# Attention and feed-forward on one core: from x stored by pairs of tokens to x stored tile by tile

## The chip, the core and the metric

The kernel runs on one core of a Trainium2 chip. The metric is device time in microseconds of one execution. Before the change the median of three runs is 562.25 us (561.91 to 562.63). Nothing leaves the core; its inputs and its output lie in HBM.

## The reference

Eight batches of 1024 tokens with 256 channels, all in fp32. What is computed, cut to what matters:

```
xn = layernorm(x)
q, k, v = split(xn @ qkv_w + qkv_b)          # 16 heads of 16 channels
q, k = l2norm(q), l2norm(k)                  # per head
kv = k^T v                                   # per head, over all tokens of a batch
attn = (q kv) @ proj_w + proj_b
ffn = relu(xn @ W1 + b1) @ W2 + b2           # 256 -> 1024 -> 256
out = x + attn + ffn
```

There is no softmax: attention is linear, so kv and proj_w are folded into one 256 x 256 matrix m per batch, and attention becomes one product of q with m.

## The kernel before, in words

**Products.** Every fp32 value is held as two parts, hi and lo, of the type that TensorE multiplies. `product` (L1097 to L1101) computes hi x hi, hi x lo and lo x hi in three matmuls, so every product below is three matmuls per chunk of 128 channels.

**Halves.** A batch is worked off in two halves of 512 tokens (`half`, s = 0 to 15, u = s mod 2), a half in four tiles of 128 tokens or two pairs of tiles. After both halves of a batch, `end` does the attention of that batch. `all_batches` writes out batch 0 and the last, and loops over those between them. The order of work is written out by hand for each engine; the engines meet through semaphores alone.

**Order of the columns.** x is transposed to channel-major form, in which a row holds one channel and a column one token. x and q are transposed in blocks of 32 x 32 on VectorE and moved by DMA (`move`) into xT_raw and qT_lo. In that form the two tiles of a pair are interleaved: the columns of the first tile are the even ones of the pair, those of the second the odd ones. Two helpers name the two views of 512 such columns: `by_tile` reads them pair, tile, token, with a step of two columns; `in_pairs` reads adjacent columns by the same three counts.

**TensorE per half.**

- `ffn_up` (j = 0 to 7): w_bank gets W1 chunk (stationary) times xT (moving, 512 columns). 6 matmuls.
- `ffn_down`: o_bank gets W2 chunk times h (moving, 512 columns). 6 matmuls. In the last half of all, `ffn_down_last` instead takes a tile of h as the stationary operand and W2 as the moving one, with 256 columns, so that the result is already token-major.
- `query_key` (t = 0 to 3): v_bank gets a tile of xT (stationary) times wqk (moving, 512 columns): q and k of 128 tokens. 6 matmuls. The tile is taken from xT by `of_tile`, every other column of a pair.
- `gather`: g_bank sums xn (stationary) times k (moving, 256 columns), 24 matmuls.

**TensorE per batch.** `key_value` and `project` make m. Then `end` runs `attend` twice (u = 0 into v_bank, u = 1 into o_bank on top of the feed-forward result): stationary m, moving qT, 512 columns, 12 matmuls each. In the last batch `attend` runs once, into w_bank, and `attend_last` uses tiles of qT (by `of_tile`) as stationaries, 256 columns.

**ScalarE and VectorE around them.** `xT_high` (L537, helper line L493) and `xT_low` (helper line L738) split xT_raw. In the opening, `xT_high_pair`, `xT_low_pair`, `xT_high_first` and `xT_low_first` split transposes that TensorE made into banks, and they write every other column to get the interleaved order. `h_high` (L568) and `h_low` (L895) split the result of the first feed-forward layer. `yT_out` (L583) copies o_bank with its bias to yT; `add_attention` (L922) adds v_bank to yT; `spread_y` (L934) transposes yT in blocks of 32 x 32 to token-major y_rows, which needs the interleaved order that the output's DMA undoes.

**Columns that the next engine waits for.** The next half's `query_key` waits for xT_lo; the next half's `ffn_down` at j = 0 waits for yT_copied of its bank; `query_key` with u = 1 waits for yT_added of v_bank.

Of the kernel before, what the change touches and what calls it, by code (L numbers as in the profile page):

```python
# [41 lines left out]
P = 128  # L42
# [20 lines left out]
def build(nc, x, qkv_w, qkv_b, proj_w, proj_b, w1, b1, w2, b2, out):  # L63
# [6 lines left out]
    with ctx:  # L70
# [155 lines left out]
        def xn_of(s):  # L226
            return xn_first[:] if is_second(s) else y_sb[:, 0] if is_third(s) else xn[:]

# [262 lines left out]
        def _(act):  # L491
# [30 lines left out]
            def xT_high_pair(a, k):  # L522

                if a == 0:
                    act.wait_ge(xT_pair_ready, k + 1)
                else:
                    act.wait_ge(xT_ready, k + 1)
                copy(xT_hi[:, 0, k, pair_tokens(a)].rearrange("f (p b) -> f b p", b=PAIR),
                     pair_banks[a][k][:, 0:PAIR * P].rearrange("f (b p) -> f b p", b=PAIR)).then_inc(
                         xT_pair_hi_done if a == 0 else xT_hi_done, 1)  # L530

            def xT_high_first(s, u, k):

                wait(act, xT_ready, KC * s + k + 1)
                copy(by_tile(xT_hi[:, u, k, :]), in_pairs(first_banks[u][k][:])).then_inc(xT_hi_done, 1)

            def xT_high(s, u):  # L537
                wait(act, x_moved, 16 * MOVES * (s - 1))
                for k in range(KC):
                    copy(xT_hi[:, u, k, :], xT_raw[:, k, :]).then_inc(xT_hi_done, 1)  # L540
# [35 lines left out]
            def yT_out(b, u, k):  # L576
# [6 lines left out]
                nc.scalar.activation(yT[u][:, k, :], o_bank[k][:], ACT.Identity,  # L583
# [151 lines left out]
        def _(dve):  # L735
# [106 lines left out]
            def xT_low_pair(a, k):  # L842

                dve.wait_ge(xT_pair_hi_done if a == 0 else xT_hi_done, k + 1)
                to, high = (t[:, 0, k, pair_tokens(a)].rearrange("f (p b) -> f b p", b=PAIR) for t in (xT_lo, xT_hi))
                less(to, pair_banks[a][k][:, 0:PAIR * P].rearrange("f (b p) -> f b p", b=PAIR), high).then_inc(
                    xT_pair_lo_done if a == 0 else xT_lo_done, 1)

            def xT_low_first(s, u, k):

                wait(dve, xT_hi_done, KC * s + k + 1)
                less(by_tile(xT_lo[:, u, k, :]), in_pairs(first_banks[u][k][:]),
                     by_tile(xT_hi[:, u, k, :])).then_inc(xT_lo_done, 1)

            def xT_low(s, u):
                for k in range(KC):
                    wait(dve, xT_hi_done, KC * s + k + 1)
                    less(xT_lo[:, u, k, :], xT_raw[:, k, :], xT_hi[:, u, k, :]).then_inc(xT_lo_done, 1)
# [59 lines left out]
            def add_attention(b, k, last):  # L918
# [3 lines left out]
                nc.vector.tensor_tensor(yT[0][:, k, :], (w_bank if last else v_bank)[k][:], yT[0][:, k, :],  # L922
                                        ALU.add).then_inc(yT_added, 1)
# [172 lines left out]
        def _(pe):  # L1096
# [50 lines left out]
            def query_key(s, u, t, batch=0):  # L1147
# [8 lines left out]
                for k in range(KC):  # L1156
                    done = product(v_bank[t % 2][:],
                                   (of_tile(xT_hi[:, u, k, :], t), of_tile(xT_lo[:, u, k, :], t)),
# [60 lines left out]
            def ffn_down_last(s, batch, j):  # L1219
# [4 lines left out]
                for t in range(TILES):  # L1224
# [4 lines left out]
                    product(to, (of_tile(h_hi[:, r, :], t), of_tile(h_lo[:, r, :], t)),  # L1229
# [158 lines left out]
```

## Time and profile before

| | us |
|---|---|
| median of three runs | 562.25 |
| the profiled execution | 562.05 |
| its span | 560.3 |
| TensorE matmul busy | 554.8 (99%) |
| TensorE weight load busy | 470.3 (84%) |
| VectorE busy | 412.5 (74%) |
| ScalarE busy | 282.5 (50%) |
| GpSimd busy | 116.7 (21%) |

The span runs from the first to the last event of the program; the execution's own time is somewhat longer. The matmul row counts matmuls from their start to a modelled end, and neighbours overlap, so their mean duration is longer than the distance between them. Weight loads (PEld) run beside matmuls.

### The profile page before, as it was taken

Reading aid. Unit: us, or ns where it says so; the run is one execution under the profiler, and the core shown is the slowest. Engines: PE = TensorE matmul, PEld = TensorE weight load, DVE = VectorE, ACT = ScalarE, POOL = GpSimd, SP = SyncE. Lnnn points to the kernel's source line nnn. Section 1 sums busy time; section 2 is a strip of 40 time slices with the busy share of each in tenths; the row PEclk is TensorE's granted clock in tenths of the full one; section 3 lists DMA queues with packets and bytes.
Section 4 is the critical chain, followed back from the end, with each engine's and each line's share of the span. In section 5 each row is a group of like instructions: output and inputs, shape, how many; then the busy total and the mean of one; then the engine's idle time right before and its main releaser. Section 6 shows DMA issues by size and latency. Waiting matters only on the chain.

```text
span 560.3 us, 8965 instructions
## 1 busy us (share of the span) xinstructions
PE 554.8 (99%) x2724; PEld 470.3 (84%) x2724; DVE 412.5 (74%) x810; ACT 282.5 (50%) x518; POOL 116.7 (21%) x148
## 2 busy tenths in 40 slices
PE   9999999999999999999999999999999999999997
PEld 7878888888888888888888888888888888888896
DVE  6787989776785867959668686876778767784745
ACT  3586373556435563365634556445554555433421
POOL 3132421502052020520214202231024300150100
PEclk9999999999999999999999999999999999999999
DMA  8422134343413434034341343414333251324412
GB/s 272 142 82 49 28 81 104 84 104 81 94 25 86 96 85 98 18 85 96 86 89 26 87 96 86 80 35 108 74 88 69 43 106 37 81 33 88 99 39 76
DMA packets 141414, 45.36 MB, mean 81 GB/s; under 512 B 133330, under 2 KB 136402, under 8 KB 141396
## 3 DMA queue, kind: packets, MB, share of 16 engines
q1 hardware_dynamic: 139280, 44.61, 34.8%
q10 hardware_dynamic: 2116, 0.53, 0.5%
q8 instruction: 9, 0.15, 0.1%
q14 instruction: 9, 0.07, 0.1%
HBM read 20.98 MB, written 8.39 MB: 52 GB/s over the span
## 4 chain that ended last, share of the span: by engine, by line
PE 96%; ACT 1%; DVE 1%; DMA 1%; SPq 0%; issue 0%; DVEq 0%
PE o_bank L1101 11%; PE o_bank L1100 11%; PE o_bank L1099 11%; PE w_bank L1099 11%; PE w_bank L1100 10%; PE w_bank L1101 10%; PE v_bank L1099 7%; PE v_bank L1101 7%; PE v_bank L1100 7%; PE g_bank L1101 3%; PE g_bank L1100 3%; PE g_bank L1099 3%; PE kv_bank L1254 1%; DMA y_sb<-w 1%; ACT xn_first L511 0%; PE kv_bank L1256 0%
## 5 line engine op out<-in xcount | busy, mean ns | idle before, releaser
L895 DVE SCALAR_TENSOR_TENSOR h_lo<-w_bank,h_hi 128x512 fp32r<-128x512 f32 x128 | 87.3, 682 | 31.8 <-ACT h_hi L568 30.3
L568 ACT ACTIVATE h_hi<-w_bank 128x512 fp32r<-128x512 f32 x128 | 76.3, 596 | 67.8 <-PE w_bank L1101 66.8
L1099 PE MATMUL w_bank<-xT_hi,w_hi 128*128 128x512 f32 x254 | 100.3, 395 | 0.0
L1100 PE MATMUL w_bank<-xT_lo,w_hi 128*128 128x512 f32 x254 | 99.2, 391 | 0.0
L1101 PE MATMUL w_bank<-xT_hi,w_lo 128*128 128x512 f32 x254 | 98.9, 389 | 0.0
L1101 PE MATMUL o_bank<-h_hi,w_lo 128*128 128x512 f32 x240 | 93.6, 390 | 0.0
L1099 PE MATMUL o_bank<-h_hi,w_hi 128*128 128x512 f32 x240 | 93.4, 389 | 0.0
L1100 PE MATMUL o_bank<-h_lo,w_hi 128*128 128x512 f32 x240 | 93.4, 389 | 0.0
L389 POOL TENSOR_TENSOR xn_lo<-xn,xn_hi 128x256 fp32r<-128x256 f32 x56 | 41.5, 741 | 220.1 <-ACT xn_hi L493 212.7
L404 POOL TENSOR_TENSOR y_sb<-y_sb,y_rows 128x256 f32<-128x256 f32 x56 | 52.2, 936 | 129.0 <-DVE y_rows L934 105.9
L546 ACT ACTIVATE qk_sq<-v_bank 128x512 f32<-128x512 f32 x64 | 38.2, 598 | 77.1 <-PE v_bank L1101 76.6
L862 DVE TENSOR_REDUCE qk_v<-qk_sq 128x32 f32<-128x512 f32 x64 | 43.2, 678 | 35.4 <-ACT qk_sq L546 35.4
L1101 PEld LDWEIGHTS w_bank<-xT_hi,w_lo 128*128 128x128 f32 x254 | 47.7, 188 | 10.5
L1099 PEld LDWEIGHTS w_bank<-xT_hi,w_hi 128*128 128x128 f32 x254 | 47.8, 188 | 9.4 <-DVE h_lo L895 0.3
L1100 PEld LDWEIGHTS w_bank<-xT_lo,w_hi 128*128 128x128 f32 x254 | 47.8, 188 | 8.8
L1099 PEld LDWEIGHTS o_bank<-h_hi,w_hi 128*128 128x128 f32 x240 | 45.1, 188 | 9.5
L1101 PEld LDWEIGHTS o_bank<-h_hi,w_lo 128*128 128x128 f32 x240 | 45.1, 188 | 9.4
L1100 PEld LDWEIGHTS o_bank<-h_lo,w_hi 128*128 128x128 f32 x240 | 45.1, 188 | 9.4
L1099 PE MATMUL v_bank<-wqk_hi,xT_hi 128*128 128x512 f32 x128 | 50.5, 395 | 0.7 <-ACT qk_even L493 0.7
L1101 PE MATMUL v_bank<-wqk_hi,xT_lo 128*128 128x512 f32 x128 | 50.5, 395 | 0.0
L1100 PE MATMUL v_bank<-wqk_lo,xT_hi 128*128 128x512 f32 x128 | 50.4, 394 | 0.0
L511 ACT ACTIVATE xn<-x_sb,ln_offset,ln_rstd 128x256 f32<-128x256 f32 x52 | 27.0, 591 | 29.5 <-DVE ln_offset L790 29.5
(203 smaller groups left out, 984.2 us busy)
## 6 DMA issues: line engine op xcount, KB each, us to landing
qT_lo<-blocks SPq DMA_DIRECT2D x256, 32.0 KB, 1.9
x_sb<-x SPq DMA_DIRECT2D x15, 512.0 KB, 3.7
y_sb<-x SPq DMA_DIRECT2D x60, 128.0 KB, 3.1
out<-y_sb SPq DMA_DIRECT2D x58, 128.0 KB, 2.5
xT_raw<-blocks SPq DMA_DIRECT2D x224, 32.0 KB, 1.9
y_sb<-w SPq DMA_DIRECT2D x4, 256.0 KB, 5.0
x_sb<-x SPq DMA_DIRECT2D x2, 256.0 KB, 2.8
w_raw<-w SPq DMA_DIRECT2D x2, 256.0 KB, 7.0
```

The costliest lines, as they stand in the source:

```text
L389: nc.gpsimd.tensor_tensor(xn_lo[:, u, t, :], xn_of(s)[:, t, :], xn_hi[:, u, t, :].bitcast(F32), ALU.subtract).then_inc(xn_split_done, 1)
L404: nc.gpsimd.tensor_tensor(y_sb[:, u, t, :], y_sb[:, u, t, :], y_rows[:, u, t, :], ALU.add).then_inc(y_done, 1)
L511: done = nc.scalar.activation(to[:, t, :], x_sb[:, u, t, :], ACT.Identity, bias=ln_offset[:, t:t + 1], scale=ln_rstd[:, t:t + 1])
L546: nc.scalar.activation(qk_sq[:, t % 2, :], v_bank[t % 2][:], ACT.Square).then_inc(qk_sq_done, 1)
L568: nc.scalar.activation(h_hi[:, j % RING, :], w_bank[j % 2][:], ACT.Relu).then_inc(h_done, 1)
L862: nc.vector.tensor_reduce(qk_v[:, t, :], qk_sq[:, t % 2, :].rearrange("p (h d) -> p h d", d=D), AXIS.X, ALU.add).then_inc(qk_ss_done, 1)
L895: nc.vector.scalar_tensor_tensor(h_lo[:, r, :], w_bank[j % 2][:], 0.0, h_hi[:, r, :].bitcast(F32), ALU.max, ALU.subtract).then_inc(h_lo_do ...
L1099: nc.tensor.matmul(to, left[0], right[0], start=first, stop=False, skip_group_check=shared)
L1100: nc.tensor.matmul(to, left[0], right[1], start=False, stop=False, skip_group_check=shared)
L1101: return nc.tensor.matmul(to, left[1], right[0], start=False, stop=last, skip_group_check=shared)
L1254: nc.tensor.matmul(kv_raw[:, g, :, :], wv_hi[:, k, heads], g_parts[:, k, :, heads], start=g == 0 and k == 0, stop=False, skip_group_check= ...
```

## The change

xT and h stand tile by tile: the 128 columns of a tile are adjacent. `xT_high` and `xT_low` now read xT_raw by tile and write adjacent columns; in the opening the split writes what the transposes gave without rearranging. `query_key` and `ffn_down_last` take a tile as 128 adjacent columns. Since h, and with it the result of the feed-forward network, now stands tile by tile and qT is still interleaved, `attend` reads its moving operand qT by tile, every other column of a pair. yT is put back in the interleaved order when it is written (`yT_out`), and `add_attention` adds in that order, so `spread_y` and the output's DMA stay as they are. `attend_last` stays as it is. The instructions of every engine are the same, in the same order and of the same size; only their access patterns differ.

```diff
             def xT_high_pair(a, k):
...
-                copy(xT_hi[:, 0, k, pair_tokens(a)].rearrange("f (p b) -> f b p", b=PAIR),
-                     pair_banks[a][k][:, 0:PAIR * P].rearrange("f (b p) -> f b p", b=PAIR)).then_inc(
-                         xT_pair_hi_done if a == 0 else xT_hi_done, 1)
+                copy(xT_hi[:, 0, k, pair_tokens(a)], pair_banks[a][k][:, 0:PAIR * P]).then_inc(
+                    xT_pair_hi_done if a == 0 else xT_hi_done, 1)
...
-                copy(by_tile(xT_hi[:, u, k, :]), in_pairs(first_banks[u][k][:])).then_inc(xT_hi_done, 1)
+                copy(xT_hi[:, u, k, :], first_banks[u][k][:]).then_inc(xT_hi_done, 1)
...
             def xT_high(s, u):
                 wait(act, x_moved, 16 * MOVES * (s - 1))
                 for k in range(KC):
-                    copy(xT_hi[:, u, k, :], xT_raw[:, k, :]).then_inc(xT_hi_done, 1)
+                    copy(in_pairs(xT_hi[:, u, k, :]), by_tile(xT_raw[:, k, :])).then_inc(xT_hi_done, 1)
...
-                nc.scalar.activation(yT[u][:, k, :], o_bank[k][:], ACT.Identity,
+                nc.scalar.activation(by_tile(yT[u][:, k, :]), in_pairs(o_bank[k][:]), ACT.Identity,
                                      bias=bias_T[:, k:k + 1]).then_inc(yT_copied, 1)
...
             def xT_low(s, u):
...
-                    less(xT_lo[:, u, k, :], xT_raw[:, k, :], xT_hi[:, u, k, :]).then_inc(xT_lo_done, 1)
+                    less(in_pairs(xT_lo[:, u, k, :]), by_tile(xT_raw[:, k, :]), in_pairs(xT_hi[:, u, k, :])).then_inc(xT_lo_done, 1)
...
-                nc.vector.tensor_tensor(yT[0][:, k, :], (w_bank if last else v_bank)[k][:], yT[0][:, k, :],
-                                        ALU.add).then_inc(yT_added, 1)
+                to = by_tile(yT[0][:, k, :])
+                nc.vector.tensor_tensor(to, in_pairs((w_bank if last else v_bank)[k][:]), to, ALU.add).then_inc(yT_added, 1)
...
             def query_key(s, u, t, batch=0):
...
-                                   (of_tile(xT_hi[:, u, k, :], t), of_tile(xT_lo[:, u, k, :], t)),
+                                   (xT_hi[:, u, k, tile(t)], xT_lo[:, u, k, tile(t)]),
...
             def ffn_down_last(s, batch, j):
...
-                    product(to, (of_tile(h_hi[:, r, :], t), of_tile(h_lo[:, r, :], t)),
+                    product(to, (h_hi[:, r, tile(t)], h_lo[:, r, tile(t)]),
...
             def attend(b, u, banks):
...
-                                       (qT_hi[:, u, g, :], qT_lo[:, u, g, :]), g == 0 and u == 0, g == KC - 1,
+                                       (by_tile(qT_hi[:, u, g, :]), by_tile(qT_lo[:, u, g, :])), g == 0 and u == 0, g == KC - 1,
```

## Rows read from the trace of the kernel before

**Rows 1.** The page, busy us, share of the span and instructions of each engine
```profile
PE 554.8 (99%) x2724; PEld 470.3 (84%) x2724; DVE 412.5 (74%) x810; ACT 282.5 (50%) x518; POOL 116.7 (21%) x148
```
**Rows 2.** The page, the chain that ended last, shares by engine
```profile
PE 96%; ACT 1%; DVE 1%; DMA 1%; SPq 0%; issue 0%; DVEq 0%
```
**Rows 3.** Waits of PE: who waited for whom, us in total, times, longest
```profile
PE w_bank L1292 <- DVE xT_raw L951: 1.1, 1, 1.1
PE v_bank L1099 <- ACT qk_even L493: 0.7, 1, 0.7
PE v_bank L1124 <- DMA y_sb<-w: 0.2, 1, 0.2
```
**Rows 4.** Stretches: length, busy us (instructions) of PE, PEld, DVE, ACT, POOL, PEclk, DMA
```profile
203.11:204.51 1.40, 1.40 (x7) 1.15 (x6) 1.40 (x3) 1.34 (x2) 0.47 (x1) 1.00 0.25 51
204.51:205.87 1.36, 1.36 (x7) 1.13 (x6) 1.36 (x3) 1.09 (x2) 1.20 (x3) 1.00 0.47 68
219.90:225.34 5.44, 5.44 (x25) 4.50 (x24) 4.14 (x7) 1.17 (x2) 0.45 (x1) 1.00 0.36 63
529.25:530.64 1.39, 1.39 (x9) 1.14 (x8) 1.39 (x2) 1.06 (x1) 0.00 (x0) 1.00 0.00 0
527.82:529.25 1.43, 1.43 (x14) 1.43 (x12) 1.43 (x2) 0.60 (x1) 0.35 (x1) 1.00 0.00 0
534.89:537.77 2.88, 2.88 (x27) 2.88 (x26) 0.09 (x1) 0.00 (x0) 0.00 (x0) 1.00 0.25 51
```
**Rows 5.** Timeline of PE around a query-key group: start us, duration us
```profile
202.88 0.39 PE L1101 MATMUL o_bank<-h_hi,w_lo 128*128 128x512 f32 x1
...
204.97 0.39 PE L1101 MATMUL w_bank<-xT_hi,w_lo 128*128 128x512 f32 x1
```
**Rows 6.** Weight loads from xT_hi and h_hi: ns min/median/max, first and last start us
```profile
L1099 PEld LDWEIGHTS w_bank<-xT_hi,w_hi x254: 186/188/192, 12.4 to 545.5; 128*128 128x128 f32 x127
...
L1099 PEld LDWEIGHTS v_bank<-wqk_hi,xT_hi x128: 193/193/195, 22.3 to 520.1; 128*128 128x128 f32 x128
...
L1099 PEld LDWEIGHTS o_bank<-w_hi,h_hi x24: 193/195/196, 527.6 to 552.9; 128*128 128x128 f32 x24
```
**Rows 7.** Matmuls that read qT_hi as moving operand, one of three forms each
```profile
L1099 PE MATMUL v_bank<-qT_hi,m_hi x28: 389/389/468, 84.4 to 492.8; 128*128 128x512 f32 x28
...
L1099 PE MATMUL o_bank<-qT_hi,m_hi x28: 389/389/390, 87.2 to 495.5; 128*128 128x512 f32 x28
...
L1099 PE MATMUL w_bank<-qT_hi,m_hi x4: 389/396/499, 548.0 to 550.2; 128*128 128x512 f32 x4
```
**Rows 8.** Groups by line and form: busy us, mean ns, idle before, releaser
```profile
L568 ACT ACTIVATE h_hi<-w_bank 128x512 fp32r<-128x512 f32 x128 | 76.3, 596 | 67.8 <-PE w_bank L1101 66.8 <-PE w_bank L1176 0.9
...
L493 ACT ACTIVATE xT_hi<-xT_raw 128x512 fp32r<-128x512 f32 x28 | 16.0, 624 | 0.6 <-DMA xT_raw<-blocks 0.6
...
L493 ACT ACTIVATE xT_hi<-kv_bank 128x512 fp32r<-128x512 f32 x1 | 0.6, 618 | 0.0
...
L738 DVE TENSOR_TENSOR xT_lo<-xT_raw,xT_hi 128x512 fp32r<-128x512 f32 x28 | 22.2, 834 | 1.9 <-ACT xT_hi L493 1.8
```
**Rows 9.** Timeline of ACT, then of DVE, at the end of a batch
```profile
224.28 0.69 ACT L583 ACTIVATE wvp_raw<-o_bank,bias_T 128x512 f32<-128x512 f32 x1 [3.90 <-DVE y_rows L934]
225.62 0.69 ACT L583 ACTIVATE wvp_raw<-o_bank,bias_T 128x512 f32<-128x512 f32 x1 [0.65 <-PE o_bank L1101]
...
222.91 0.69 DVE L922 TENSOR_TENSOR xn_first<-v_bank,xn_first 128x512 f32<-128x512 f32 x1 [0.66 <-PE v_bank L1101]
...
226.99 1.97 DVE L738 TENSOR_TENSOR xT_lo<-xT_raw,xT_hi 128x512 fp32r<-128x512 f32 x2
```
**Rows 10.** Timeline of PE, the same place: the products that need those results
```profile
226.70 0.39 PE L1099 MATMUL o_bank<-h_hi,w_hi 128*128 128x512 f32 x1
...
227.38 0.39 PE L1099 MATMUL o_bank<-h_hi,w_hi 128*128 128x512 f32 x1
...
230.78 0.39 PE L1099 MATMUL v_bank<-wqk_hi,xT_hi 128*128 128x512 f32 x1
```

More of the change, by code:

```diff
@@ L844, in xT_low_pair @@
                 dve.wait_ge(xT_pair_hi_done if a == 0 else xT_hi_done, k + 1)
-                to, high = (t[:, 0, k, pair_tokens(a)].rearrange("f (p b) -> f b p", b=PAIR) for t in (xT_lo, xT_hi))
-                less(to, pair_banks[a][k][:, 0:PAIR * P].rearrange("f (b p) -> f b p", b=PAIR), high).then_inc(
-                    xT_pair_lo_done if a == 0 else xT_lo_done, 1)
+                to, high = (t[:, 0, k, pair_tokens(a)] for t in (xT_lo, xT_hi))
+                less(to, pair_banks[a][k][:, 0:PAIR * P], high).then_inc(xT_pair_lo_done if a == 0 else xT_lo_done, 1)
             def xT_low_first(s, u, k):
                 wait(dve, xT_hi_done, KC * s + k + 1)
-                less(by_tile(xT_lo[:, u, k, :]), in_pairs(first_banks[u][k][:]),
-                     by_tile(xT_hi[:, u, k, :])).then_inc(xT_lo_done, 1)
+                less(xT_lo[:, u, k, :], first_banks[u][k][:], xT_hi[:, u, k, :]).then_inc(xT_lo_done, 1)
             def xT_low(s, u):
```

## The prediction

> **What bounds the kernel now.** I read the page from the top. The first lines give each engine's busy time: TensorE's matmul row is busy for 554.8 of 560.3 us, the next engine, VectorE, for 412.5 [rows 1]. The chain that ended last is matmul for 96% of the span [rows 2]. The table of waits for that engine holds three entries, 2.0 us in all, one each at the start of the program, none in the loop over batches [rows 3]. So the time is the number of matmuls times the distance from one start to the next, plus a start and a tail of a few us. The granted clock of TensorE is 1.00 in all the stretches that I use (the 2.4 GHz level) [rows 4]. What a matmul costs is therefore not its "mean ns" (about 390, with overlapping ends) but the distance of starts. That is read from stretches that begin and end on a start, divided by the matmuls between them [rows 4]:
> - attention, 24 products of 512 columns, adjacent stationary columns, adjacent moving columns: 5.44 us, 226.7 ns each;
> - the first feed-forward product, six: 1.36 us, 226.7 ns each;
> - query-key, six, the same 512 moving columns, stationary columns two apart: 1.40 us, 233.3 ns each.
>
> The single starts show the edges too: from the last matmul before a query-key group to the third start after it are nine distances, 202.88 to 204.97, 2.09 us against 9 x 226.7 = 2.04 [rows 5]. The weight loads tell the two kinds apart: median 188 ns where the columns are adjacent, 193 for all 256 query-key loads that the hi part gives [rows 6].
>
> **What the change removes.** Query-key stationaries become adjacent. There are 16 halves of a batch with 4 token tiles, so 64 groups of six products (k = 2, three products each), 384 matmuls. Inside a group 6 x 6.6 = 40 ns, with the edges about 50; I take 45 ns: 64 x 0.045 = **2.9 us**, all of it on the path, since nothing but the previous matmul holds the next one. The bounds of this term are 2.5 (no edges) and 3.2 us. Zero would need the cause to be something else than the stride (a rival below).
>
> The last half's second feed-forward product also has stationaries two apart, 96 matmuls of 256 columns, which become adjacent. Their loads take 195 ns, but twelve starts lie 1.43 us apart, 119 ns each, and the 24 products of the gather beside them, with adjacent columns, take 2.88 us, 120 ns each [rows 4, 6]. At 256 columns the stride costs nothing, so this edit is worth 0. The 24 attention products of the last half keep their strided stationaries.
>
> **What it adds.** Attention now reads its moving operand qT in steps of two columns: 24 products in each of seven batches and 12 in the last, 180 matmuls of 512 columns [rows 7]. No matmul of this program reads a strided moving operand, so I bound the price X of one:
> - below, 0: the stride disappears, as it does in the 256-column rows above;
> - nearest row, 6.6 ns: a stationary read at the same step of 8 bytes, in a product of the same width [rows 4];
> - above, one column in two cycles instead of one: another 512 / 2.4 = 213.3 ns.
>
> I take the nearest row, 6.6 ns: 180 x 6.6 = **1.2 us** lost. A gain below 0 is excluded, because contiguous is the easiest order to read. The sum on TensorE is 1.2 - 2.9 = -1.7 us.
>
> The Trainium skill (Advanced Engine Details and Errata, section SBUF Cachelines; also SBUF — State Buffer, section Specifications (TRN2)) says that SBUF has lines of 16 bytes and that two hits on a line suffice to absorb its latency. Two fp32 columns a step of 8 bytes apart do share a line, so by that rule neither strided operand costs anything, and the sum would be 0. The trace disagrees with it for the stationary side: 233.3 against 226.7 ns.
>
> **What it moves on the other engines.** No instruction is added, removed or put elsewhere; only patterns of reading and writing change.
> - xT_hi and xT_lo from xT_raw read at a step of two and write adjacently; 624 and 834 ns a piece now [rows 8]. The pair of subtractions that starts at 226.99 takes 1.97 us and ends at 228.96; the query-key product that needs it starts at 230.78 [rows 9, 10]: 1.8 us of cover, so the pair could all but double.
> - yT written back in pair order (ScalarE, L583): the second one, of the last bank, runs 225.62 to 226.31, and the feed-forward product that overwrites that bank starts at 227.38, the one on the first bank at 226.70 after an ACT end at 224.97 [rows 9, 10]. Cover 1.1 and 1.7 us, for a write whose step of two I price by the one such write in the opening: 618 ns, against 596 for a plain read of a bank [rows 8], some 20 ns.
> - adding the attention to yT (VectorE, L922) ends 223.60, its bank is needed at 230.78: 7 us of cover.
> - the opening's pair copies lose their strided write; a saving like the 20 ns above, on two of them in a row, is under 0.1 us. Taken as 0.
>
> If one of these covers went, ScalarE would be late with the next h_hi, and the first feed-forward products after attention would wait.
>
> **Sum.** The profiled execution took 562.05 us (span 560.3 and 1.75 around it), the median of three is 562.25. 562.05 - 1.7 = 560.35, and against the median **560.5 us**, 0.3% faster. A measurement of this kernel can tell about 0.2%, 1.1 us, from no change.
>
> **Rivals.**
> 1. *The strided moving read is free.* For it: the 256-column rows, where a strided load changes nothing, and the rule on two hits a line, taken for the moving side alone (the Trainium skill, as above). Against it: the same stride shows in the same width on the other operand. Time: 562.25 - 2.9 = 559.3 us. Chance 0.24.
> 2. *Each moving product pays its fixed surplus twice.* A matmul of 512 columns takes 226.7 ns where 512 columns at 2.4 GHz are 213.3; 13.4 ns come on top. If that is the weight load's reading getting in the way of the stream, a stream that touches twice as many places could pay it twice: 180 x 13.4 = 2.4 us, -0.5 in all, 561.7 us. Against it: a load with twice the places raised the 13.4 by 6.6 only. The Trainium skill (TensorE: Matmul & The Clock Gate, step by step) gives the two operands a read port each, which speaks against it as well. Chance 0.14.
> 3. *Slower: the stream pays by the column.* The stationary has 128 columns and costs 6.6 ns more; the moving operand has 512, and if the price goes with their number, it is 4 x 6.6 = 26.4 ns a matmul, 180 x 26.4 = 4.8 us, +1.9 in all: 564.1 us. The mechanism decides from X = 2.9 / 180 = 16 ns upwards. For it: the moving side takes 512 columns in 213 ns, twice the pace of a load that brings 128 in the 120 ns between starts of the 256-column rows, so it has less room for a slower read. Chance 0.14.
> 4. *The same place, its extreme: half the pace.* If steps of 8 bytes let only one column in every two cycles, 180 x 213.3 = 38.4 us, less 2.9: 597.7 us. Against it: the load with that step has lost 5 ns on 188, not half its pace. But the load never had to run at the stream's pace [rows 4, 6]. Chance 0.12.
> 5. *The change does not do what it says*: the 6.6 ns are not the stride's. For it: six feed-forward products right after narrow ones take 1.39 us, 231.7 ns each, with adjacent columns [rows 4], so the distance has other causes as well. Against it: every strided load is longer than its neighbours, by 5 ns and more, before 512 columns and before 256 [rows 6]. Then the gain is 0, and with a free moving read the time stays 562.3. Chance 0.05.
>
> **How the numbers follow.** The forecast has 0.31. The time is its own, 560.5. The low end is rival 1 with the larger bound of the gain, 558.9; the high end takes in rivals 2, 3 and 5 with half a us for their sizes, 564.6. Only rival 4, and what falls outside by its size, is left out. Faster by over 0.2%: forecast and rival 1, 0.55 (X below 10 ns). Within: rivals 2 and 5, 0.19. Slower: rivals 3 and 4, 0.26. As both signs hold much of the chance, the forecast's own range is 559.9 to 561.1.
>
> **What would show it.** Right: query-key loads at 188 ns, six products in 1.36 us; attention's 24 products in 5.60 us (233.3 each), feed-forward unchanged at 226.7; waits of TensorE still some 2 us. Rival 1: attention still 5.44. Rival 2: 5.76. Rival 3: 6.07. Rival 4: over 10. Rival 5: query-key still 1.40. A new wait of the matmul row on ScalarE's o_bank copies or on xT_lo in the loop would prove the covers wrong.

## The result, and the profile after

The changed kernel takes 600.34 us (median of four runs, 600.15 to 601.22), against 562.44 us for the kernel before on the same chip: ratio 1.0676, 95% interval 1.0663 to 1.0688. The change costs 37.9 us. The time lies outside the range of the prediction; it is near that of rival 4, 597.7.

The page of the changed kernel, busy time of each engine, and the shares of the chain that ended last (they answer to [rows 1, 2]):

```profile
PE 592.2 (99%) x2724; PEld 471.0 (79%) x2724; DVE 410.0 (69%) x810; ACT 284.5 (48%) x518; POOL 117.7 (20%) x148
...
PE 91%; DVE 3%; ACT 3%; issue 1%; DMA 1%; SPq 0%; POOL 0%; DVEq 0%; ACTq 0%; POOLq 0%
```

TensorE's matmul row grew by 37.4 us, nearly the whole loss. All other rows stand within 2.5 us of where they were. The chain is still mostly matmul; the small entries are the opening.

The waits of TensorE (who waited for whom, us in total, times, longest), answering to [rows 3]:

```profile
PE w_bank L1291 <- DVE xT_raw L950: 1.1, 1, 1.1
PE v_bank L1098 <- ACT qk_even L495: 0.8, 1, 0.8
PE w_bank L1175 <- ACT xT_hi L495: 0.5, 1, 0.5
```

Three entries, 2.4 us in all where there were 2.0, and all in the opening; no new wait in the loop. So the 37 us are not time in which TensorE waited for something. Each product must take longer. Stretches of the changed kernel (length; busy us and instructions of PE, PEld, DVE, ACT, POOL; PEclk; DMA share and GB/s), answering to [rows 4]: the 24 attention products of a batch, then the six query-key products of a tile, then six of the first feed-forward product:

```profile
229.87:240.73 10.86, 10.86 (x25) 4.96 (x24) 4.61 (x7) 1.27 (x2) 2.92 (x4) 1.00 0.25 38
246.21:247.57 1.36, 1.36 (x8) 1.13 (x6) 1.36 (x3) 0.00 (x0) 1.14 (x2) 1.00 0.00 0
247.57:248.93 1.36, 1.36 (x8) 1.13 (x6) 1.36 (x2) 1.08 (x2) 0.00 (x0) 1.00 0.09 19
```

Attention's 24 products took 5.44 us and now take 10.86: 452.5 ns each, +225.8. Query-key went from 1.40 to 1.36, 226.7 each. The feed-forward product beside it is where it was. The granted clock is 1.00 in all three, so the clock is not the cause. The starts in the timeline show it product by product (start us, modelled duration us):

```profile
229.65 0.39 PE L1100 MATMUL o_bank<-h_hi,w_lo 128*128 128x512 f32 x1
229.87 0.61 PE L1098 MATMUL v_bank<-qT_hi,m_hi 128*128 128x512 f32 x1
230.31 0.63 PE L1099 MATMUL v_bank<-qT_lo,m_hi 128*128 128x512 f32 x1
```

The step from 0.22 us between starts to 0.44 comes exactly at the first product that reads qT in steps of two columns.

The sum over the whole program: 180 attention products at +226 ns are 40.7 us; the query-key groups give back some 2.9 (the forecast's figure; 64 groups at 0.04 us in these stretches are 2.6 without the edges); 562.05 + 40.7 - 2.9 = 599.9, where the profiled execution took 600.15. The other matmuls after the opening add up to the same time as before within 0.2 us. Among them are the 96 narrow products of the last half, whose stationaries also became adjacent: 120.9 ns apart before, 121.1 after.

Groups of ScalarE and VectorE whose patterns changed (busy us, mean ns, idle before and its releaser), answering to [rows 8]. First the kernel before, the copy to yT:

```profile
L583 ACT ACTIVATE wvp_raw<-o_bank,bias_T 128x512 f32<-128x512 f32 x14 | 9.6, 689 | 33.0 <-DVE y_rows L934 23.4 <-PE o_bank L1101 9.6
```

Then the changed kernel:

```profile
L495 ACT ACTIVATE xT_hi<-xT_raw 128x512 fp32r<-128x512 f32 x28 | 17.0, 659 | 0.0
...
L584 ACT ACTIVATE wvp_raw<-o_bank,bias_T 128x512 f32<-128x512 f32 x14 | 10.0, 716 | 70.4 <-PE o_bank L1100 70.4
```

```profile
L739 DVE TENSOR_TENSOR xT_lo<-xT_raw,xT_hi 128x512 fp32r<-128x512 f32 x28 | 21.9, 823 | 1.8 <-ACT xT_hi L495 1.7
```

A strided read adds 35 ns to ScalarE's xT_hi (624 before), a strided write 27 ns to yT (689 before). It adds nothing to VectorE's subtraction (823 after, 834 before). The long idle time before L584 is a follower: it waits for attention, which ends later, and TensorE's table shows no wait for it.

### The profile page after: what moved, and what is told of

It reads as the page before. It is cut to its first block, busy times and chain, and to the rows that moved or that the text cites. A ratio compares the mean times of both kernels' runs of the same rounds, so it can differ in the third digit from the quotient of the medians.

```text
span 598.4 us, 8965 instructions
## 1 busy us (share of the span) xinstructions
PE 592.2 (99%) x2724; PEld 471.0 (79%) x2724; DVE 410.0 (69%) x810; ACT 284.5 (48%) x518; POOL 117.7 (20%) x148
## 4 chain that ended last, share of the span: by engine, by line
PE 91%; DVE 3%; ACT 3%; issue 1%; DMA 1%; SPq 0%; POOL 0%; DVEq 0%; ACTq 0%; POOLq 0%
PE o_bank L1100 11%; PE o_bank L1099 11%; PE o_bank L1098 11%; PE w_bank L1098 10%; PE w_bank L1099 9%; PE w_bank L1100 9%; PE v_bank L1098 7%; PE v_bank L1100 6%; PE v_bank L1099 6%; PE g_bank L1100 3%; PE g_bank L1099 3%; PE g_bank L1098 3%; DMA w_raw<-w 1%; PE kv_bank L1253 1%; DVE ln_parts L767 0%
## 5 line engine op out<-in xcount | busy, mean ns | idle before, releaser
L584 ACT ACTIVATE wvp_raw<-o_bank,bias_T 128x512 f32<-128x512 f32 x14 | 10.0, 716 | 70.4 <-PE o_bank L1100 70.4
```

Of the source, the lines that this page charges most:

```text
L584: nc.scalar.activation(by_tile(yT[u][:, k, :]), in_pairs(o_bank[k][:]), ACT.Identity, bias=bias_T[:, k:k + 1]).then_inc(yT_copied, 1)
```

## The experiments

### Is it attention's read alone?

The theory: the whole loss is 226 ns for each product with a strided moving operand, and the rest of the change is worth what was forecast. The rival: part of the loss hangs on the new patterns of the other engines, or on the combination. Three kernels divide the change.

**e1: everything but attention's read.**

```diff
-                                       (by_tile(qT_hi[:, u, g, :]), by_tile(qT_lo[:, u, g, :])), g == 0 and u == 0, g == KC - 1,
+                                       (qT_hi[:, u, g, :], qT_lo[:, u, g, :]), g == 0 and u == 0, g == KC - 1,
```

> The changed kernel, with attention reading qT in adjacent columns again; it leaves out the reordering of attention's columns, all else is the change. Theory (the step of the moving operand costs 226 ns on each of 180 products, 40.7 us, and nothing else in the change costs anything): 600.3 - 40.7 = 559.6 us, 2.9 us or 0.5% under the kernel before, attention's starts 226.7 ns apart. Rival (a part of the 37.9 us lies elsewhere, in the writes of yT in pair order or in the strided reads of xT_raw by ScalarE and VectorE): the time stays above 562 by that part.

Measured: 559.47 us (559.28 to 559.65) against 562.39, ratio 0.9947 (0.9932 to 0.9963). The same stretch of this kernel, the 24 attention products:

```profile
219.09:224.53 5.44, 5.44 (x26) 4.51 (x25) 4.11 (x7) 1.26 (x2) 0.45 (x1) 1.00 0.42 72
```

It is the old 5.44 us. The gain of the adjacent stationaries, 2.9 us, is real and arrives in full. The new patterns on ScalarE and VectorE add nothing to the time.

**e2: attention's read alone, in the kernel before.**

```diff
-                                       (qT_hi[:, u, g, :], qT_lo[:, u, g, :]), g == 0 and u == 0, g == KC - 1,
+                                       (by_tile(qT_hi[:, u, g, :]), by_tile(qT_lo[:, u, g, :])), g == 0 and u == 0, g == KC - 1,
```

> The kernel before, with one edit alone: attention reads qT every other column (its columns come in another order than those they are added to). Theory (the strided moving read is the whole loss, and the gain of query-key is apart from it): 562.4 + 40.7 = 603.1 us, query-key still at 233.3 ns between starts, attention at 452.7. Rival (the doubling needs the rest of the change, such as qT read beside strided writes of yT): well under 603, near 562 in the extreme.

Measured: 602.85 us (602.79 to 604.33), ratio 1.0718 (1.0701 to 1.0734). That is 40.5 us for 180 products, 225 ns each. The two parts, -2.9 and +40.5, add up to the change's 37.9 within 0.3.

**e3: the strided read in half of the products** (the first half of each batch reads adjacent columns, into its own bank).

```diff
-                to = by_tile(yT[0][:, k, :])
-                nc.vector.tensor_tensor(to, in_pairs((w_bank if last else v_bank)[k][:]), to, ALU.add).then_inc(yT_added, 1)
+                nc.vector.tensor_tensor(yT[0][:, k, :], (w_bank if last else v_bank)[k][:], yT[0][:, k, :],
+                                        ALU.add).then_inc(yT_added, 1)
...
-                                       (by_tile(qT_hi[:, u, g, :]), by_tile(qT_lo[:, u, g, :])), g == 0 and u == 0, g == KC - 1,
+                                       tuple(by_tile(q[:, u, g, :]) if u else q[:, u, g, :] for q in (qT_hi, qT_lo)), g == 0 and u == 0, g == KC - 1,
```

> The changed kernel, but the attention of the first half of each batch goes into its own bank, so it reads qT adjacently there and the bank is added to yT in pair order; only the second half's 84 products read every other column. Theory (226 ns for each strided product, no fixed cost): 559.6 + 84 x 0.226 = 578.6 us. Rival (a fixed price of changing from one kind of read to the other, or a price that comes from long rows of such products): not half-way, near 560 or near 600.

Measured: 579.45 us (two runs, 579.16 and 579.74), ratio 1.0302 (1.0283 to 1.0321). Against e1, 84 strided products seem to cost 20.0 us, 238 ns each. The profiled executions tell where the excess over 226 lies: the distances of attention's products add up to 18.9 us more than in e1, 225 ns for each of the 84, and the first attention product starts at 85.52 us instead of 84.36, in a stretch in which the two kernels are the same. The timeline of TensorE shows the pace change at the bank, within one attention:

```profile
228.22 0.39 PE L1100 MATMUL v_bank<-qT_hi,m_lo 128*128 128x512 f32 x1
228.45 0.61 PE L1098 MATMUL o_bank<-qT_hi,m_hi 128*128 128x512 f32 x1
228.89 0.63 PE L1099 MATMUL o_bank<-qT_lo,m_hi 128*128 128x512 f32 x1
```

So the price belongs to the read, product by product; it came in v_bank and in o_bank, and whether the product in front was strided or not.

### What does a moving read cost, by its pattern?

Each kernel of this section and the next was run once. Nothing is read from their total times; what counts is the distance of starts in the trace, at a stated clock, which comes back in one batch after another within a few ns.

**p1.** The attention products read eight patterns of columns from W1 instead of qT, one pattern for each three products, same instructions otherwise.

```diff
+                return (w[:, 0:512], w[:, 0:1024:2],
+                        w[:, 0:1536:3], w[:, 0:2048:4],
+                        w[:, 0:1024].rearrange("p (n s e) -> p n s e", s=2, e=2)[:, :, 0],
+                        w[:, 1:1025].rearrange("p (n s e) -> p n s e", s=2, e=2)[:, :, 0],
+                        w[:, 0:1024].rearrange("p (n s e) -> p n s e", s=2, e=4)[:, :, 0],
+                        w[:, 0:512].rearrange("p (a b n) -> p b a n", a=2, b=2))[2 * n + g]
```

> The changed kernel with attention's moving operand taken from the weights W1, which stand still, in eight patterns of 512 columns, one for each product of two chunks, in this order: adjacent; every 2nd column; every 3rd; every 4th; two adjacent of four, beginning at column 0; the same beginning at column 1; four adjacent of eight; and adjacent runs of 128 in changed order. The result of attention is left out. Theory A (half the pace comes from the step of two columns itself: the stream is read in pairs of adjacent columns, 8 bytes a cycle at half of 2.4 GHz, and a pair with one useful column brings one): every 2nd, 3rd and 4th column all 452, two of four from column 0 at 227, from column 1 more than 227, runs at 227. Theory B (it goes by lines of 16 bytes that are touched): every 2nd 452, every 3rd and 4th longer still, up to 900; two of four 452, four of eight 227. Theory C (it goes by the number of dimensions of the pattern): every 2nd, 3rd and 4th in two dimensions 227, the runs in changed order 452.

Measured: 586.43 us (one run). The eight stretches of one batch, three products each, in the order of the patterns above (columns as before):

```profile
226.43:227.11 0.68, 0.68 (x4) 0.56 (x3) 0.68 (x2) 0.55 (x1) 0.00 (x0) 1.00 1.26 209
227.11:228.45 1.34, 1.34 (x4) 0.60 (x3) 0.62 (x1) 0.00 (x0) 0.00 (x0) 1.00 1.22 186
228.45:229.81 1.36, 1.36 (x4) 0.62 (x3) 0.69 (x1) 0.00 (x0) 0.00 (x0) 1.00 0.01 2
229.81:231.19 1.38, 1.38 (x4) 0.62 (x3) 0.00 (x0) 0.00 (x0) 0.00 (x0) 1.00 0.00 0
231.19:232.59 1.40, 1.40 (x5) 0.63 (x3) 1.09 (x2) 0.00 (x0) 0.00 (x0) 1.00 0.00 0
232.59:233.94 1.35, 1.35 (x4) 0.62 (x3) 0.81 (x2) 0.00 (x0) 0.46 (x1) 1.00 0.00 0
233.94:234.66 0.72, 0.72 (x5) 0.58 (x3) 0.00 (x0) 0.41 (x1) 0.64 (x2) 1.00 0.00 0
234.66:235.35 0.69, 0.69 (x4) 0.56 (x3) 0.23 (x1) 0.33 (x1) 0.62 (x2) 1.00 0.00 0
```

Adjacent: 227 ns a product. Every second, third and fourth column: 447, 453 and 460 (the first product of the second columns is short, the other two take 450 and 452). Two adjacent of four: 467 (452 from column 1 on). Four adjacent of eight: 240, its second and third products 228 and 232. Whole runs of 128 columns in another order: 231. So it is not the pattern's complexity that costs; groups of four adjacent fp32 columns (16 bytes) are all it takes for nearly full pace, and one or two of four halve it. Steps of 8, 12 and 16 bytes cost practically the same. None of the three theories fits whole: A wanted two of four from column 0 at 227, C wanted the steps at 227 and the runs at 452, and B, by lines of 16 bytes, has the groups right but wanted more than 452 for every third and fourth column.

**p2.** The same place with other patterns: a bf16 operand read adjacent and at steps of 2, 4 and 8 columns (each repeated to fill 512), then fp32 at a step of eight, adjacent from column 1, each column twice, and a product of 256 columns at a step of two.

```diff
+                if n < 4:
+                    moving = (narrow[:, 0:512], narrow[:, 0:1024:2], again(narrow[:, 0:1024:4], 2),
+                              again(narrow[:, 0:1024:8], 4))[n]
+                    weights, moving = (narrow[:, 0:P],) * 2, (moving,) * 2
+                elif n == 4:
+                    moving = tuple(again(w[:, 0:1024:8], 4) for w in moving)
...
+                else:
+                    to, moving = to[:, 0:256], tuple(w[:, 0:512:2] for w in moving)
```

> As the run before, other patterns, and what attention computes is left out: with bf16 operands (a tile set to 0.5) 512 adjacent columns; every 2nd; every 4th of 1024 twice; every 8th of 1024 four times; then with the fp32 parts every 8th of 1024 four times; adjacent from column 1; each of 256 columns twice in a row; and every 2nd column with 256 columns only. If the pace goes by bytes read in pairs of 8 bytes, bf16 at every 2nd column (4 bytes) stays at about 216 to 227 and at every 4th and 8th (8 and 16 bytes) doubles; if it goes by the step not being 1, bf16 doubles at every 2nd already. fp32 every 8th: 452 by pairs, more by lines. From column 1: 227 or little more. Each column twice: 227 if a repeated column stays in the pair, 452 if only an adjacent step counts. 256 columns with step 2: 2 x 106.7 and a surplus, about 226, where 120 is the distance without a step.

Measured: 592.06 us (one run). bf16: 216 ns adjacent, 226 at 4 bytes, 452 at 8, 899 at 16. Behind three products of the last kind the granted clock fell, so that most of the fp32 patterns stood at another clock than meant. Stretches: from the start of the last bf16 product on, then the fp32 products at 0.50, then the last two products of 256 columns (columns as before):

```profile
231.60:232.90 1.30, 1.30 (x3) 0.52 (x2) 0.09 (x1) 0.00 (x0) 0.00 (x0) 0.74 0.00 0
232.90:234.20 1.30, 1.30 (x4) 0.92 (x3) 1.30 (x3) 0.00 (x0) 0.00 (x0) 0.50 0.00 0
234.20:235.48 1.28, 1.28 (x4) 0.99 (x3) 0.51 (x1) 0.09 (x1) 0.69 (x1) 0.50 0.00 0
236.20:236.66 0.46, 0.46 (x3) 0.42 (x2) 0.30 (x1) 0.03 (x1) 0.38 (x2) 1.00 0.00 0
```

At a granted clock of 0.50, the level of 1.2 GHz, these fp32 patterns take 416 to 432 ns: every eighth column 431 and 432, adjacent from column 1 and each column twice 416 to 427. 512 columns at 1.2 GHz are 427 ns, so at that level a step of eight adds next to nothing. Back at 1.00, the 256 columns at a step of two take 229 ns (120 without a step, [rows 4]), nearly the same doubling as for 512.

**p3.** The fp32 patterns again, with one that tells two theories apart. H: fp32 has two paces alone, full with four adjacent columns, half otherwise. L: the price is the number of 16-byte lines that the read touches.

```diff
+                    moving = tuple((w[:, 1:513],
+                                    w[:, 2:1026].rearrange("p (n s e) -> p n s e", s=2, e=4)[:, :, 0],
+                                    again(w[:, 0:1024:4], 2), None,
+                                    w[:, 0:512],
+                                    w[:, 0:256].unsqueeze(2).to_broadcast([P, 256, 2]),
+                                    w[:, 0:2048].rearrange("p (n s e) -> p n s e", s=4, e=2)[:, :, 0],
+                                    again(w[:, 0:1024:8], 4))[n] for w in moving)
```

> The changed kernel with attention's moving operand from W1 in other patterns, and attention's result left out, in this order: adjacent from column 1; four adjacent of eight from column 2, across lines of 16 bytes; every 4th of 1024 columns, twice; bf16 every 8th of 1024 (16 bytes) four times; adjacent; each of 256 columns twice in a row; two adjacent of eight; every 8th of 1024 fp32 columns four times. Theory L (the stream gets 0.6 lines of 16 bytes a ns; a line touched costs as much however much of it is used): from column 1 227; four of eight across lines 452 or less; every 4th 850; bf16 every 8th 900; each twice 227; two of eight 452; every 8th 850. Theory H (fp32 has two paces alone, full where groups of four adjacent columns fill a line, half elsewhere, as every 2nd, 3rd and 4th column gave 452 to 460): from column 1 227 or 452, four of eight across lines 452, every 4th 452 to 460, two of eight 452, every 8th 452 to 460, each twice 452.

Measured: 601.14 us (one run). Four of its stretches: adjacent from column 1; four of eight from column 2, so that each group of four crosses a line; every fourth column; every eighth (32 bytes):

```profile
230.39:231.10 0.71, 0.71 (x5) 0.56 (x3) 0.71 (x2) 0.55 (x1) 0.00 (x0) 1.00 1.16 200
231.10:232.45 1.35, 1.35 (x5) 0.60 (x4) 0.59 (x1) 0.00 (x0) 0.00 (x0) 1.00 1.02 178
232.45:233.83 1.38, 1.38 (x4) 0.42 (x3) 0.69 (x1) 0.00 (x0) 0.00 (x0) 1.00 0.01 1
...
239.25:240.54 1.29, 1.29 (x4) 0.62 (x3) 0.52 (x1) 0.00 (x0) 1.13 (x3) 1.00 0.00 0
```

Four of eight across the lines: 450 ns, where the aligned groups of p1 took some 230. So it is 16-byte lines, not runs of four, that count; a contiguous read from column 1 takes 237, since all but its ends are whole lines. But every fourth and every eighth column, a line for each column, take 460 and 430, not twice that. L falls for them; H holds. H missed in one pattern: with each column twice it expected 452, and the products took 216. Two adjacent of eight took 457 on average and bf16 every eighth 898, which are L's figures as well.

In the batch at 302 us the clock fell behind the bf16 products, and two adjacent of eight ran at 0.50:

```profile
310.86:312.27 1.41, 1.41 (x4) 0.96 (x3) 0.20 (x1) 0.74 (x1) 1.31 (x2) 0.50 0.00 0
```

That is 468 ns a product, where each column twice took 421 to 427 just in front of it, at the same 0.50. So the read keeps its price at half the clock; only the pace of the columns changes with the clock.

**p4.** bf16, 128 columns read four times over, steps of 1 to 8 columns.

```diff
+                moving = again(narrow[:, 0:P * (n + 1):n + 1], 4)
+                weights, moving = (narrow[:, 0:P],) * 2, (moving,) * 2
```

> The changed kernel with attention's operands replaced by bf16 ones set to 0.5, its result left out: 128 columns four times over, in the eight products of two chunks with steps of 1, 2, 3, 4, 5, 6, 7 and 8 columns (2 to 16 bytes). If the price goes by lines of 16 bytes touched, at 0.6 lines a ns, the distance grows with every step over 2: 216, 226, 320 to 347, 427 to 452, 533, 640, 747, 853 to 900. If it goes by fixed paces, there are plateaus: 216 to 227 for steps up to 2, 452 from 3 to 4, and 900 from some step on.

Measured: 620.95 us (one run). The first product of the steps 1, 2, 4 and 8 in the timeline of TensorE (the modelled duration holds the step as well):

```profile
236.59 0.39 PE L1100 MATMUL v_bank<-narrow 128*128 128x512 bf16 x1
...
237.24 0.39 PE L1100 MATMUL v_bank<-narrow 128*128 128x512 bf16 x1
...
238.93 0.62 PE L1100 MATMUL v_bank<-narrow 128*128 128x512 bf16 x1
...
246.36 1.08 PE L1100 MATMUL o_bank<-narrow 128*128 128x512 bf16 x1
```

From product to product inside each step: 216, 226, 340, 451, 564, 675, 788 and 899 ns. From the second step on the price is 112.5 ns times the step, without plateaus. 128 bf16 columns at a step of s touch 16 s lines, four times over 64 s: 1.76 ns a line, in every step.

In this batch the clock fell at 245.7 us, between products of 788 ns. Two products of step 7, at 1.00, and two of step 8, at 0.50:

```profile
243.99:245.57 1.58, 1.58 (x3) 0.23 (x2) 0.43 (x1) 0.71 (x1) 1.42 (x3) 1.00 0.00 0
246.36:248.16 1.80, 1.80 (x3) 0.25 (x2) 0.00 (x0) 0.00 (x0) 0.00 (x0) 0.50 0.00 0
```

The 899 ns of step 8 at 0.50 are the 899 that p2 measured at 1.00; step 7 took 788 at 0.50 as well (p4, batch at 160 us). The price of a line is a time, not a number of TensorE's cycles.

### Does the stationary operand follow the same rule?

**s1.** In the kernel before, query-key reads its stationaries at steps of 1, 2, 3 and 4 columns, one step for each tile.

```diff
-                                   (of_tile(xT_hi[:, u, k, :], t), of_tile(xT_lo[:, u, k, :], t)),
+                                   (xT_hi[:, u, k, 0:(t + 1) * P:t + 1], xT_lo[:, u, k, 0:(t + 1) * P:t + 1]),
```

> The kernel before, with query-key's stationaries taken as adjacent columns (first tile of four), every 2nd (second), every 3rd (third) and every 4th (fourth); other tokens than the right ones, so q and k are another computation. Theory (a stationary read with a step costs 6.6 ns once the step is not 1, since the load never has to run at the stream's pace): 226.7, 233.3, 233.3, 233.3. Rival (by lines of 16 bytes touched: 32, 64, 96, 128 lines): 226.7, 233, 240, 247 or so, and weight loads of 188, 193, 199, 204 ns.

Measured: 562.72 us (one run). Six products at a step of 2, of 3 and of 4:

```profile
203.48:204.87 1.39, 1.39 (x7) 1.16 (x6) 1.19 (x2) 1.39 (x3) 0.20 (x1) 1.00 0.23 47
207.60:209.01 1.41, 1.41 (x7) 1.40 (x6) 1.06 (x2) 0.71 (x2) 0.28 (x1) 1.00 0.69 189
212.68:214.09 1.41, 1.41 (x7) 1.40 (x6) 0.72 (x2) 0.00 (x0) 0.00 (x0) 1.00 0.28 58
```

and the first weight load of each, in the timeline:

```profile
203.48 0.19 PEld L1099 LDWEIGHTS v_bank<-wqk_hi,xT_hi 128*128 128x128 f32 x1
...
207.61 0.25 PEld L1099 LDWEIGHTS v_bank<-wqk_hi,xT_hi 128*128 128x128 f32 x1
...
212.69 0.31 PEld L1099 LDWEIGHTS v_bank<-wqk_hi,xT_hi 128*128 128x128 f32 x1
```

The loads grow, from 188 ns (step 1) and 193 to 252 and 309, more than any theory had put down. But they run beside the stream of 512 columns, and the distance of products stays at 232 to 235. The load has slack that the stream hasn't; this is why its 6.6 ns say nothing about the moving side.

The loads themselves fit the rule of the moving side. 128 fp32 columns touch 64, 96 and 128 lines at the steps 2, 3 and 4, and the loads grow by 59 and 57 ns, 1.8 ns for each line more. At p4's price 128 lines take 225 ns, still no longer than the stream's 227. This was read off afterwards, and no run has such loads beside narrower products. By the same price 96 lines take 169 ns, more than the 120 ns between products of 256 columns: an estimate from these rows is that a step of three would cost there.

### Can the gain be kept?

The gain of e1 needs q tile by tile too. Its split on ScalarE and VectorE can put it so, at no price on TensorE, if the raw q lies in another buffer than qT_lo (the subtraction in place can't reorder).

**e4: a buffer of its own.** There was room for half a batch only, by sharing small buffers (and adding the biases on GpSimd earlier), so the move of the next q waits for the split of this one, and the first split is done one step earlier.

```diff
+        qT_raw = sb("qT_raw", [P, KC, HALF])
...
+                wait(sp, qT_lo_done, s)
+                move(q_blocks, qT_raw[:], q_moved)
...
-                    copy(qT_hi[half], qT_lo[half].bitcast(F32)).then_inc(qT_hi_done, 1)
+                    copy(in_pairs(qT_hi[half]), by_tile(qT_raw[:, k])).then_inc(qT_hi_done, 1)
...
                 if is_second(s):
+                    qT_low(0, 0)
                     transpose_q(s, u)
```

> The changed kernel, with q's columns put tile by tile where they are split: the DMA brings q into a raw tile of its own, ScalarE and VectorE read that one every other column and write adjacent ones, so TensorE reads nothing with a step. Space comes from the identity and the signs lying in kv's tile and one norm tile less; q of the first half is split one step earlier. Theory (strided reads are free for ScalarE and VectorE, and cost only on TensorE): 562.4 - 2.9 = 559.5 us, all products of 512 columns 226.7 ns apart, but for those after narrow ones. Rival (the single raw tile makes q's DMAs wait for the split before, and they push x's DMAs behind them, or the opening's earlier split delays the first keys): 560 to 563, with a new wait of the matmul row for qT_lo or xT_lo.

Measured: 560.99 us (nine runs, 560.70 to 562.61), ratio 0.9976 (0.9966 to 0.9986): 1.4 us gained, half of what was expected. A wait of TensorE that was not there says why (the profiled execution is the slowest of the nine, 562.61, 3.2 us over e1's: 1.6 by this stop, and about 1 by a gap at 30.5 us, which the profiled execution of e2 shows too, with the opening of the kernel before):

```profile
PE w_bank L1100 <- DVE h_lo L897: 1.5, 1, 1.5
```

It stands at 75.5 us, in the second half of the first batch. The 1.6 us of the earlier split (VectorE, 67.66) stand in front of the next layernorm there, xn and its transposes come later, and the first feed-forward product with them. That the split's place is the cause is read from this order; it was not tried apart.

**e5: raw q in the rows of y.** y_rows is free between the output of one batch and the attention of the next, and has room for both halves.

```diff
+        qT_raw = [y_rows[:, u].rearrange("p t c -> p (t c)").rearrange("p (k n) -> p k n", k=KC) for u in range(2)]
...
-                move(q_blocks, qT_lo[:, u].bitcast(F32), q_moved)
+                move(q_blocks, qT_raw[u], q_moved)
...
                 wait(dve, q_moved, 16 * MOVES * s)
+                wait(dve, y_done, TILES * (s - 1))
```

> As the run with q's columns put tile by tile at the split, but the DMA brings q raw into y_rows of the same half, which lies idle until the batch's end; so the two halves have a raw tile each, no DMA waits for a split, and the opening's order is that of the change. VectorE's transpose of q waits for the sums of y_rows before (done some 2 us earlier in the trace of before). Theory (only the wait that the single raw tile brought, 1.5 us on the matmul row in the opening, kept that run from its 559.5): 559.5 us, 0.5% under the kernel before, no new wait of the matmul row. Rival (strided reads on ScalarE and VectorE, or q's split, cost something on the path in every batch): 560.5 or more.

Measured: 563.37 us (eight runs, 561.78 to 564.33) against 561.98, ratio 1.0022 (1.0011 to 1.0034). It missed: the gain is gone and more. The wait of TensorE, and then the chain behind it in the timelines of VectorE, GpSimd and SyncE's queue:

```profile
PE g_bank L1101 <- DVE k_lo L740: 2.0, 1, 2.0
```

```profile
98.05 1.30 DVE L831 STREAM_TRANSPOSE blocks<-qk_even 128x512 f32<-128x512 f32 x2 [3.50 <-POOL y_sb L407]
```

```profile
94.83 7.18 POOL L407 TENSOR_TENSOR y_sb<-y_sb,y_rows 128x256 f32<-128x256 f32 x8 [18.80 <-DMA y_sb<-x]
```

```profile
78.69 10.62 SPq L328 DMA_DIRECT2D xT_raw<-blocks  x16
89.43 4.44 SPq L312 DMA_DIRECT2D y_sb<-x  x8
```

The transpose of q now needs y done. In the first batch y waits for the load of x into y_sb, whose eight issues stand behind sixteen of the move of x. TensorE stopped for some 2.2 us (2.40 between two starts). What came behind the stop cost more time. Two stretches of `gather`, products of 256 columns, some 0.7 us and 4 us behind it:

```profile
102.40:105.50 3.10, 3.10 (x16) 3.10 (x16) 2.81 (x14) 0.20 (x1) 0.00 (x0) 0.50 0.19 37
105.64:106.11 0.47, 0.47 (x6) 0.47 (x5) 0.23 (x2) 0.09 (x1) 0.00 (x0) 1.00 0.20 39
```

Behind the stop the granted clock was 0.50, and 16 products took 213 ns instead of 118: another 1.5 us. Not every execution paid this: the two of the eight with a mean clock of 1.000 took 561.78 and 562.77 us, the six with 0.996 or 0.997 took 563.21 to 564.33.

**e6: the same, with the first loads of y issued before the moves.**

```diff
+                first = isinstance(b, int) and b == 0
+                if first:
+                    sp.wait_ge(x_transposed, 1)
+                    sp.wait_ge(xn_split_done, 3 * TILES)
+                    load_y(b, 0, last)
                 move_q(s, u)
...
-                    for loaded_half in range(2):
+                    for loaded_half in range(int(first), 2):
```

> As e5_q_raw_in_y_rows, with one load moved: in the first batch SyncE issues the four loads of y's first half before it moves q of the second half, where its queue stands idle, instead of 25 us later behind x's moves. Theory (the 3.5 us for which VectorE waited for the sums of y_rows at 98 us, once, and the 2.4 us of the matmul row behind it are all that the run before lost): GpSimd sums the first half by 93 us, VectorE does not wait, 559.5 us, 0.5% under the kernel before. Rival (later batches lose as well, where the sums end close to the transpose of q): above 560.5, with waits of VectorE for y_sb in the loop.

Measured: 559.98 us (nine runs, 559.44 to 561.64) against 562.10, ratio 0.9964 (0.9953 to 0.9975). The waits of TensorE:

```profile
PE w_bank L1296 <- DVE xT_raw L955: 1.1, 1, 1.1
PE v_bank L1103 <- ACT qk_even L498: 0.9, 1, 0.9
PE w_bank L1180 <- ACT xT_hi L498: 0.6, 1, 0.6
PE w_bank L1103 <- DVE h_lo L899: 0.2, 1, 0.2
```

The stop is gone, and with it 3.4 us against e5. This version leaves nothing out and is faster than both kernels: by 2.1 us (0.4%) than the one before, by 40 than the change. That is 0.8 us short of e1's gain of 2.9.

## Why the prediction was wrong

**What bounds the kernel** was right: TensorE's matmul row bounds it before and after, and the time is a sum over distances of starts. That is why the error of one term went into the time in full.

**What it removes** was right in sign, size and place. e1 has this part alone: 559.47, a gain of 2.9 us as forecast. Rival 5, that the 6.6 ns are not the stride's, has fallen with it. That the edit of the last half is worth nothing shows in the two traces, 120.9 and 121.1 ns between those products.

**What it moves on the other engines** was right: e1 contains all of it but attention's read, with no new wait. The price of a strided write on ScalarE was put at 20 ns and is 27.

**What it adds** is the step that failed: "I take the nearest row, 6.6 ns". X is 226 ns, 34 times as much; the term is 40.7 us instead of 1.2. The row was near in name (the same step, the same width of product), but not in what counts. It belongs to a load that brings 128 columns beside a stream of 512; s1 shows that such a load can grow by 121 ns while the distance grows by only 8. A moving read has no such slack. The prediction knew the argument, "the load never had to run at the stream's pace", yet left it in rival 4 with a chance of 0.12, and rival 4 outside the range. The argument is one on whether the row may be used at all, and belonged to the choice of X: without that row the bounds were 0 and 213 with nothing between to lean on, and the range would have had to reach at least 597.7. Even that would have been 2.6 us short: the upper bound, 213.3, put the second cycle of each column on top of an unchanged surplus of 13.4 ns, and the measured distance, 452.5, is twice the whole 226.7. (The low end, 558.9, is 562.05 - 3.2, from the profiled execution; from the median it is 559.05. Nothing hangs on it.)

**Rival 4** was right in place and nearly in size: 213.3 ns against 226. Its mechanism, one column in every two cycles, is not what the runs show: at half the clock it would give 853 ns, and two adjacent of eight took 468 there (p3), bf16 at 14 and 16 bytes the same 788 and 899 ns at either level (p2, p4). **Rival 3**, a price by the column of 26.4 ns in all, had part of the reason (the moving side has less room for a slower read) and a size taken from the same wrong row. **Rivals 1 and 2** fell with the first stretch.

Rival 1 leaned on a sentence of the Trainium skill (Advanced Engine Details and Errata, section SBUF Cachelines): "Need at least two hits on a cacheline to absorb SRAM access latency". The prediction read it as saying that two suffice. That reading is not borne out here for the moving operand: with two fp32 columns of each line used the products take 452 ns, with four 227. In bf16, where a line has eight columns, four hits take 226, two take 451 and one takes 899.

## What to carry to other kernels

The moving operand of a matmul should use whole 16-byte lines, four adjacent fp32 columns or more at a time; where an order of columns must be changed, do it in a pass of ScalarE or VectorE that runs anyway (27 to 35 ns on 128x512 for ScalarE here and nothing for VectorE's subtraction, against 226 ns for each product that reads the result). A stride on the stationary operand is cheap beside a stream of 512 columns, 6.6 ns a product at a step of two and some 8 at four, since the load runs beside the stream. A price is to be taken from a row only if the operation there had to keep the same pace; if it had slack, it bounds nothing.

## What the runs showed of the hardware

- **One price for each line.** All bf16 distances, and the fp32 ones from two columns a line upwards, fit 1.76 ns for each 16-byte line that the moving read touches within 6%: 128 lines 226 ns, 256 lines 451, 512 lines 899. (The first product of a pattern can stand 3 to 4% lower, and of four adjacent of eight it took 255.) Even the adjacent pair of 216 (bf16, or fp32 with each column twice: 64 lines for 512 columns) and 227 (fp32: 128 lines) fits, the first held by the columns (213.3 ns), the second by the lines. This was read off after p4; no run was made to test it.
- **fp32 below two columns a line is better than that**: every third, fourth and eighth column take 453, 460 and 431 ns, not 676 or 899. Why is open.
- **The read does not slow down with TensorE's clock.** With 1.2 GHz granted, the columns alone take 427 ns for 512, and a pattern whose lines take longer keeps its own time: two adjacent of eight 468 ns (457 at 2.4 GHz), bf16 at a step of 14 bytes 788 and at 16 bytes 899 at both levels. So at the lower clock a step costs only what its lines take beyond 427 ns. The change's own pattern, every second column, was not seen at that level.
- **In four of these runs the granted clock fell before the last product**: behind a stop of 2.2 us (e5); at or behind three products of 899 ns in seven of the eight batches of p2 and in five of p3; and in seven batches of p4, from products of 675 to 788 ns on, for 7 to 10 us. In p2, p3 and p4 the matmul row read as fully busy. A busy row does not by itself keep the clock up. The stop of 1.5 us in e4 left it at 1.00.
